# A fused conditional residual kernel: a new order of the work on all five engines

## What is computed

```
x = x + (softmax(mask(tanh(x W1 + b1) v)) x) / count        # attention pooling, A = 128
x = x + layernorm(x + relu(x w1[lang] + b1) w2[lang] + b2[lang]) * gamma[lang] + beta[lang]
x = x + zX * lap_columns(x) + zY * lap_rows(x) + zR * x * (1 - x)
x = x + x W[cat] + b[cat]                                   # W[cat]: 512 x 512, 1 MB
```

## Time and profile before

| what | value |
|---|---|
| median of 3 runs | 1118.82 us (1113.79 to 1120.64) |
| the profiled execution | 1114.18 us, span 1112.4 us |
| PE busy | 1051.4 us, 95% |
| DVE busy | 961.6 us, 86% |
| POOL busy | 710.2 us, 64% |
| ACT busy | 495.7 us, 45% |

### The profile page before, as it was taken

The page is one execution under the profiler, slowest core; times in us unless marked ns, Lnnn a source line. Parts: engine busy times, 40 slices in busy tenths (PEclk is TensorE's granted clock), DMA queues, the critical chain, the costliest instruction groups (busy, mean ns, idle before and its releaser), DMA issues.

```text
span 1112.4 us, 23554 instructions
## 1 busy us (share of the span) xinstructions
PE 1051.4 (95%) x4892; PEld 658.1 (59%) x4892; DVE 961.6 (86%) x1965; ACT 495.7 (45%) x1410; POOL 710.2 (64%) x652
## 2 busy tenths in 40 slices
PE   2489999999999999999999999999999999999996
PEld 1356665665666556666666656665666565565652
DVE  3288998998899889999899999988998898998984
ACT  0244444444444444444454444444444444444441
POOL 0066667657667676667667666666766766766765
PEclk9999999999999999999999999999999999999999
DMA  9478888788888988877787778898888788888873
GB/s 382 179 219 260 272 244 257 235 235 236 281 247 237 308 257 265 233 212 228 237 249 223 224 233 266 254 276 242 253 246 259 234 264 249 273 267 219 251 232 113
DMA packets 136182, 273.95 MB, mean 246 GB/s; under 512 B 29288, under 2 KB 29296, under 8 KB 128496
## 3 DMA queue, kind: packets, MB, share of 16 engines
q1 hardware_dynamic: 97600, 202.45, 60.2%
q10 hardware_dynamic: 38448, 70.01, 20.8%
HBM read 248.26 MB, written 33.55 MB: 253 GB/s over the span
## 4 chain that ended last, share of the span: by engine, by line
issue 32%; POOL 31%; PE 24%; DVE 9%; DMA 2%; DVEq 1%; POOLq 0%; ACT 0%; ACTq 0%; SPq 0%
POOL b_wide L817 12%; PE ps_out L390 10%; POOL neighbours L798 7%; POOL react L804 6%; POOL rstd L790 4%; DVE x L709 4%; PE bank_hidden L344 3%; PE ps_attn L322 3%; PE ps_adapt L372 3%; PE ps_pool L363 2%; DVE res L684 2%; DMA xts<-in_xT 2%; POOL above L810 2%; PE ps_x3T L380 1%; PE bank_scores L333 1%
## 5 line engine op out<-in xcount | busy, mean ns | idle before, releaser
L390 PE MATMUL ps_out<-w3s,x3T 128*128 x1024 | 489.5, 601 | 2.3 <-ACT x3T L441 2.3
L810 POOL TENSOR_TENSOR above<-above,below 128x512 f32<-128x512 f32 x128 | 164.6, 1286 | 255.8 <-DMA above<-x 255.3
L390 PEld LDWEIGHTS ps_out<-w3s,x3T 128*128 128x128 f32 x1024 | 185.2, 191 | 189.7 <-issue 188.1
L709 DVE SCALAR_TENSOR_TENSOR x<-above,zy_t,react 128x512 f32<-128x512 f32 x128 | 209.4, 1636 | 10.5 <-POOL above L810 8.9
L804 POOL TENSOR_TENSOR react<-react,x 128x512 f32<-128x512 f32 x128 | 179.8, 1405 | 2.1 <-ACT react L484 2.1
L817 POOL TENSOR_TENSOR b_wide<-b_wide,x 128x512 f32<-128x512 f32 x128 | 178.0, 1391 | 1.8 <-DMA b_wide<-in_b 1.8
L344 PE MATMUL bank_hidden<-w_all,xts 128*128 x1024 | 137.7, 278 | 23.6 <-DMA xts<-in_xT 23.6
L344 PEld LDWEIGHTS bank_hidden<-w_all,xts 128*128 128x128 f32 x1024 | 125.1, 193 | 54.1 <-issue 52.4
L790 POOL TENSOR_TENSOR rstd<-var_eps,minus_half 128x1 f32<-128x1 f32 x128 | 69.9, 546 | 133.1 <-DVE var_eps L676 133.1
L462 ACT ACTIVATE square_junk<-ps_adapt,neg_mean 128x512 f32<-128x512 f32 x128 | 88.0, 688 | 133.7 <-DVE neg_mean L639 133.7
L372 PE MATMUL ps_adapt<-w_all,hid 128*128 x256 | 133.6, 604 | 12.5 <-DVE x L691 12.1
(11 more groups left out here) (97 smaller groups left out, 1252.1 us busy)
## 6 DMA issues: line engine op xcount, KB each, us to landing
w3s<-in_w SPq DMA_DIRECT2D x128, 1024.0 KB
xts<-in_xT ACTq DMA_DIRECT2D x128, 256.0 KB, 4.9
xs<-in_x ACTq DMA_DIRECT2D x128, 256.0 KB, 5.4
b_wide<-in_b SPq DMA_DIRECT2D x128, 256.0 KB, 4.7
out_x<-res SPq DMA_DIRECT2D x128, 256.0 KB, 3.3
below<-x SPq DMA_DIRECT2D x128, 252.0 KB
above<-x SPq DMA_DIRECT2D x128, 252.0 KB
below<-x SPq DMA_DIRECT2D x256, 2.0 KB
```

What stands on the lines that cost most here:

```text
L390: mm = pe.matmul(ps_out[j.ring(2)][:, :], x3T[:, j.ring(2), k * P:(k + 1) * P], w3s[:, bass.ds(wslot * (K * D) + k * D, D)], start=(k == 0 ...
L709: nc.vector.scalar_tensor_tensor(x3[:, q, :], above[:, q, :], zy_t[:, bass.ds(i.n, 1)], react[:, q, :], ALU.mult, ALU.add).then_inc(x3_rea ...
L810: nc.gpsimd.tensor_tensor(above[:, q, :], above[:, q, :], below[:, q, :], ALU.add).then_inc(rows_ready, 1)
```

## The change

Nothing is added to or taken from the work of the engines; what changes is the order in `slot` on all five, and with it how many slots lie between a step and its use. On PE attn_project(s) comes first and takes over the wait for the transposed item, the category product is split into steps 0 and 1 at the end of one slot and steps 2 and 3 early in the next, mix_transpose is one slot later than its scores, and adapter_up stands after pool and the x3 transposes. adapter_project now waits for the relu of the item just before, and adapter_hidden for its own item's xw. On ACT load_xT(s) is the first step of slot s instead of a step of slot s-1. On DVE normalize stays last, with add_rows right before it, add_columns comes early and one item later, add_beta late, result one item later. On POOL the slot begins with inverse_std. On SP the shifts come first, then the b3 load of the item before, the store one item later, and the category load last.

```diff
@@ -269,16 +269,18 @@
 
             def slot(s):
                 if s.inside(B):
+                    shift_rows(s)
+                if (s - 1).inside(B):
+                    cat_m1, = load_params(sp, CAT, 1, s - 1)
+                    load_b3(s - 1, cat_m1)
+                if (s - 3).inside(B):
+                    item_m3, = load_params(sp, ITEM, 1, s - 3)
+                    store(s - 3, item_m3)
+                if s.inside(B):
                     cat, fresh, wslot = load_params(sp, CAT, 3, s)
-                    shift_rows(s)
                     load_w3(s, cat, fresh, wslot)
-                if (s - 2).inside(B):
-                    item_m2, = load_params(sp, ITEM, 1, s - 2)
-                    store(s - 2, item_m2)
-                if s.inside(B):
-                    load_b3(s, cat)
-
-            run_slots(slot, 0, B + 1)
+
+            run_slots(slot, 0, B + 2)
             for r in range(2):
                 sp.wait_ge(res_out[r], 16 * (B // 2))
                 sp.wait_ge(w3_in[r], 16 * (B // 2))
@@ -314,6 +316,7 @@
 
             def attn_project(a):
                 r = a.ring(2)
+                pe.wait_ge(xT_in[r], a.dma())
                 if a.is_first:
                     pe.wait_ge(w1a_in, 16)
                 if a.is_at_least(1):
@@ -335,11 +338,10 @@
                           ).then_inc(scores_mm, 1)
 
             def adapter_project(s, lang):
-                pe.wait_ge(xT_in[s.ring(2)], s.dma())
                 if s.is_first:
                     pe.wait_ge(w1_in, 16)
-                if s.is_at_least(2):
-                    pe.wait_ge(relu_ready, s.upto(2))
+                if s.is_at_least(1):
+                    pe.wait_ge(relu_ready, s.upto(1))
                 for k in range(K):
                     mm = pe.matmul(ps_xw, xts[:, s.ring(2), k, :], w1_all[:, bass.ds(lang * (K * A) + k * A, A)],
                                    start=(k == 0), stop=(k == K - 1))
@@ -350,8 +352,7 @@
                 pe.transpose(ps_mixT, mix[:, c.ring(2), :], ident[:, :]).then_inc(mixT_mm, 1)
 
             def adapter_hidden(f):
-                if (f + 1).inside(B):
-                    pe.wait_ge(xw_ready, (f + 1).upto())
+                pe.wait_ge(xw_ready, f.upto())
                 pe.wait_ge(mixT_ready, f.upto())
                 pe.matmul(ps_hid, xw[:, f.ring(2), :], mixT[:, f.ring(2), :], start=True, stop=True
                           ).then_inc(hid_mm, 1)
@@ -393,36 +394,35 @@
                     mm.then_inc(out_mm, 1)
 
             def slot(s):
-                h, j = s - 1, s - 4
-                if h.inside(B):
-                    pool(h)
-                if s.inside(B):
-                    kind, = load_params(pe, KIND, 1, s)
+                h, i, j = s - 1, s - 4, s - 5
+                if s.inside(B):
+                    attn_project(s)
+                if h.inside(B):
+                    mix_transpose(h)
                 if j.inside(B):
                     wslot, = load_params(pe, WSLOT, 1, j)
-                if h.inside(B):
+                    category(j, wslot, range(2, K))
+                if s.inside(B):
+                    kind, = load_params(pe, KIND, 1, s)
+                if h.inside(B):
+                    adapter_hidden(h)
+                if s.inside(B):
+                    attn_scores(s, kind)
+                if h.inside(B):
+                    pool(h)
                     lang_m1, = load_params(pe, LANG, 1, h)
-                if s.inside(B):
-                    attn_scores(s, kind)
-                if j.inside(B):
-                    category(j, wslot, range(0, 1))
+                if i.inside(B):
+                    x3_transpose(i)
                 if h.inside(B):
                     adapter_up(h, lang_m1)
-                if j.inside(B):
-                    category(j, wslot, range(1, K))
-                if (s + 1).inside(B):
-                    lang_p1, = load_params(pe, LANG, 1, s + 1)
-                if s.inside(B):
-                    mix_transpose(s)
-                if (s + 1).inside(B):
-                    adapter_project(s + 1, lang_p1)
-                    attn_project(s + 1)
-                if (s - 3).inside(B):
-                    x3_transpose(s - 3)
-                if s.inside(B):
-                    adapter_hidden(s)
-
-            run_slots(slot, -1, B + 3)
+                if s.inside(B):
+                    lang, = load_params(pe, LANG, 1, s)
+                    adapter_project(s, lang)
+                if i.inside(B):
+                    wslot_next, = load_params(pe, WSLOT, 1, i)
+                    category(i, wslot_next, range(0, 2))
+
+            run_slots(slot, 0, B + 4)
 
 
         @block.scalar
@@ -517,32 +517,31 @@
                 act.dma_start(xs[:, r], x[bass.ds(item, 1)].rearrange("o s d -> s (o d)")).then_inc(x_in[r], 16)
 
             def slot(s):
+                if s.inside(B):
+                    item, = load_params(act, ITEM, 1, s)
+                    load_xT(s, item)
+                if (s - 2).inside(B):
+                    lang_m2, = load_params(act, LANG, 1, s - 2)
+                    relu(s - 2, lang_m2)
                 if (s - 1).inside(B):
                     exponentials(s - 1)
+                if (s - 5).inside(B):
+                    move_x3T(s - 5)
+                if s.inside(B):
+                    load_x(s, item)
                 if (s - 3).inside(B):
                     reaction(s - 3)
-                if (s + 1).inside(B):
-                    item_p1, = load_params(act, ITEM, 1, s + 1)
-                    load_xT(s + 1, item_p1)
+                if (s - 2).inside(B):
+                    variance(s - 2)
                 if (s - 3).inside(B):
                     column_ends(s - 3)
-                if s.inside(B):
-                    item, = load_params(act, ITEM, 1, s)
-                    load_x(s, item)
-                if (s - 2).inside(B):
-                    variance(s - 2)
                 if (s - 1).inside(B):
+                    move_xw(s - 1)
                     move_mixT(s - 1)
                 if s.inside(B):
-                    move_xw(s)
                     attn_tanh(s)
-                if (s - 4).inside(B):
-                    move_x3T(s - 4)
-                if (s - 1).inside(B):
-                    lang_m1, = load_params(act, LANG, 1, s - 1)
-                    relu(s - 1, lang_m1)
-
-            run_slots(slot, -1, B + 3)
+
+            run_slots(slot, 0, B + 4)
 
 
         @block.vector
@@ -730,30 +729,30 @@
                     row_max(s)
                 if h.inside(B):
                     add_b2(h, lang)
+                if (s - 3).inside(B):
+                    add_columns(s - 3)
+                if s.inside(B):
+                    denominator(s)
+                if h.inside(B):
+                    add_adapted(h)
+                if s.inside(B):
+                    row_scale(s)
+                if h.inside(B):
+                    mean(h)
+                if s.inside(B):
+                    mix_rows(s)
+                if (s - 5).inside(B):
+                    result(s - 5)
+                if h.inside(B):
                     add_beta(h, lang)
-                if s.inside(B):
-                    denominator(s)
-                if h.inside(B):
-                    add_adapted(h)
-                if s.inside(B):
-                    row_scale(s)
-                if h.inside(B):
-                    mean(h)
-                if s.inside(B):
-                    mix_rows(s)
+                    add_epsilon(h)
+                    center(h, lang)
                 if (s - 3).inside(B):
                     add_rows(s - 3)
-                if (s - 4).inside(B):
-                    result(s - 4)
-                if h.inside(B):
-                    add_epsilon(h)
-                    center(h, lang)
-                if (s - 2).inside(B):
-                    add_columns(s - 2)
                 if h.inside(B):
                     normalize(h)
 
-            run_slots(slot, 0, B + 3)
+            run_slots(slot, 0, B + 4)
 
 
         @block.gpsimd
@@ -818,18 +817,17 @@
                                         ).then_inc(x3_b3_ready, 1)
 
             def slot(s):
+                if s.inside(B):
+                    inverse_std(s)
+                    sum_columns(s)
                 if (s - 2).inside(B):
-                    sum_rows(s - 2)
+                    add_b3(s - 2)
                 if (s - 1).inside(B):
-                    sum_columns(s - 1)
-                if (s - 3).inside(B):
-                    add_b3(s - 3)
-                if (s - 1).inside(B):
-                    react_times_x2(s - 1)
-                if s.inside(B):
-                    inverse_std(s)
-
-            run_slots(slot, 0, B + 2)
+                    sum_rows(s - 1)
+                if s.inside(B):
+                    react_times_x2(s)
+
+            run_slots(slot, 0, B + 1)
 
 
```

(18 more changed lines are left out.)

4 lines of the change are left out of this document (2 added, 2 removed).

## The result

The changed kernel takes 1196.93 us in the median of 4 runs (1190.72 to 1204.69), the one before 1119.59 beside it: 1.07 times as long, with a 95% interval of 1.0648 to 1.0751. The forecast was 1100, with a range up to 1122.

What follows compares the result with a forecast made beforehand. TensorE was taken as the bound, 8.04 us a slot, losing 19.9 us to DVE's order. 1114.2 - 25.7 = 1088.5; + 3.5 (xT) + 5.5 (b3, lock) = 1097.5, plus about half of 4.6: 1100 us, range 1088 to 1122.

Steps and rivals of the forecast that it cites:

- the frame of the change part by part: New slot timed from attn_project's start on PE; SP and PE load one index more, PE's floor stays 8.04 us.
- The b3 chain: SP's late b3 load delays POOL's add_b3; free in most slots, at its edge behind a new category.
- rival 3: b3 chain costs 0.4 us in each of 55 slots: 1114, or 1105 to 1110; 0.23 shared by three rivals.
- the lock: DVE and POOL instructions exclude each other: add_rows gains 1.0 us, add_columns and mix lose up to 1.0 each.
- The walk: Step-by-step timing of the new slots; over four slots 8.95, 7.6, 7.2 and 7.6 us, mean 7.8.
- The 19.9 us: TensorE's loss over 122 loop slots, read from adapter_up's wait for DVE's normalize; the change was to remove it.
- The floor: Sum of TensorE's work in one slot, 8.04 us, every piece kept by the change.
- The sum without losses: 1114.2 less 25.7 us for loop, head and tail: 1088.5, before the xT, b3 and lock costs.
- The room of adapter_up: On PE, normalize ends 1.7 us before adapter_up needs it, now about 0.5; its wait under 4 us in all.
- The xT load: load_xT issued later, landing free up to 6.2 us before attn_project on PE stops; 3.5 us taken.
- rival 1: xT becomes the bound: slot 8.45 us at a typical landing of 6.6, about 1138 us; chance 0.11.
- rival 2: DVE becomes the bound, two locks in every slot, 8.24 us: about 1113; 0.23 shared by three rivals.

Runs made afterwards that it cites:

- e9: Changed kernel with two whole copies for the six shifts and b3 loaded for the first two items only: 1090.85 us, ratio 0.9755.
- e5: Changed kernel with one parameter load per slot on SP instead of three: 1130.68 us, ratio 1.0137.
- e12: Changed kernel with one parameter load per slot on SP, three b3 buffers and load_b3 ahead of the shifts: 1097.26 us, ratio 0.9786.
- e4: Kernel before with two whole copies of 128 rows for the six shifts: 1100.86 us, ratio 0.9842.
- e14: Kernel before with two whole copies for the six shifts and b3 loaded for the first two items only: 1097.71 us, ratio 0.9808.
- e6: Kernel before with one parameter load per slot on SP instead of two: 1107.64 us, ratio 0.9931.
- e10: Kernel before with one parameter load per slot and four shifts (127 rows and one edge row each way) instead of six: 3289.86 us, ratio 2.9438.
- e7: Kernel before with one parameter load per slot on SP and the four one-row shifts issued by ACT: 1154.79 us, ratio 1.0388.

## Why the prediction was wrong

**The step that failed** is in the frame of the change part by part: "SP and PE load one index more per slot, in their sequencers", at a price of nothing. For PE that holds: with its extra load it reaches 8.04 a slot in e9, with nothing lost. SP does nothing but load and issue, and there the load counts in full; the statement ahead of the prediction that nothing is added to the work of the engines leaves it out too (384 parameter loads on SP for 256). SP's slot was never summed: 606.76 to 614.44 is 7.68, and the mean without waits 8.06, with two loads in it that no row of the forecast showed. With the third it is 8.57, and 122 x (8.57 - 8.04) = 65 us; 54 to 66 by the runs. What was taken was the issue time of the six shifts, as a delay of b3 inside a slot, not as a share of a stream that repeats.

The Trainium skill (DMA: Bandwidth & Descriptors, "Latency and other measured facts") gives `tensor_load` a floor of some 600 ns. On SP the median here is 716, which bears the size out, but the least is 266, under that floor, and there the measurement decides. As an estimate from the page's figure, the third load would have made SP's 8.06 into 8.7.

**The b3 chain** (rival 3) was seen with its right mechanism and undersized. It was put at 5.5 us with the lock, 22 at most. In e5, where SP has time, the loop loses 35.8, and the third buffer takes 30.7 of them away (e12). The walk had SP stand in load_w3's wait, start the shifts at 3.8 and issue b3 8.6 to 9.2 us into a slot. In the slot after the one above, attn_project starts at 658.52 by PE's timeline, x2 ends at 3.6 instead of 2.6, the shifts start at 5.2 (663.69), and b3, of 669.19, is at 10.7. SP is hardly ever in load_w3's wait (3.2 us in the whole loop): it comes to the shifts late from its own stream, the last parameter load of 1.28 in front. Landings were within (4.1 in the median; 7.97 in the stall above, issued at 580.86), but they came on top of an issue that was already late.

**The 19.9 us** were read as the cost of DVE's order, with adapter_up's wait as the proof. e4 and e14 refute that: with the old order and two copies for the shifts, 12 and 15.5 of them are gone, and that wait falls from 12.1 to 1.7 and 1.4. DVE's x2 was late since the shifts were late, two steps back: POOL's 255.3 us of waits for them fall to 24.0 and 4.1. The wait named the last link, not the first. SP's length alone explains only a part (4.9 in e6, where the six issues between x2 and the last shifted row stay). What the new order adds where SP and b3 are out of the way is small: e9 stands 6.9 us below e14, with intervals that just part; the four waits for the mix at the head (7.6 us in e14) are gone, as forecast.

**What was right.** The floor: 8.04 a slot, reached in e9. The sum without losses, 1088.5, stands against 1093.32 in e9's profiled execution: loop and tail come out as summed, and the 4.8 between are the head, where item 5's mix transpose is at 80.24 and not at 75.4, hardly sooner than before. The room of adapter_up: 0.8 us of waits in e12, forecast under 4. The xT load: PE waits 6.5 us for it in the loop, 3.5 were taken. In e5 it is PE's largest wait in the loop (9.6 us), but in e9 and e12 nothing is left of it there, so rival 1 falls. DVE's busy time of 901, under 962 and far from rival 2's 1010, with add_rows at its least of 0.74 in most items of e12. attn_project(1) at 42.13 against 42.2. Half right: item 5's mix transpose at 78.17 against 75.4, half the gain. Not as said: add_columns stays at 0.744 in the median, where 1.2 was expected, since POOL often stands idle beside it, waiting for b3; in e12 it is 0.946. And the forecast's own sign of being wrong, a usual slot above 8.15, came: 8.30. The tail took 35.3 us from the last mix transpose to the end, 31.3 were forecast: it is 30.6 in e12, so b3 and SP are late there too, though no run takes the tail apart.

**The miss in one line:** of the 98.8 us between the sum of 1097.5 and the profiled execution's 1196.3, 92 lie in the loop (a loss of 100.2, where 9.0 were allowed less 0.9 for the last item), 3 at the head, 4 at the tail.

## What to carry to other kernels

Sum the stream of every engine against the slot, and of the engine that only issues above all: its DMA issues (0.35 to 0.9 us each), its register loads and its arithmetic stand in no line of busy times. An engine at 8.06 us a slot beside a TensorE of 8.04, with few waits, is a second bound, and the first thing that a change of order must not lengthen. When a transfer is asked for at the end of a long stream and waits for its buffer, a third buffer and an earlier place can be worth more than a finer order of the engines that compute: here 33 us (e5 to e12) against 7 (e14 to e9).

## What the runs showed of the hardware that was not expected

- Rows decide the price of a shift out of proportion: the old order with the single load takes 1107.64 us with 126 rows (e6) and 3289.86 with 127 (e10), and rows come up to 21.9 us late. The price doesn't show at the issue of the first 127 rows (0.74 us) but at the two issues behind it (7.82 and 11.91), the latter of one row. The Trainium skill (DMA: Bandwidth & Descriptors, "Why a DMA increments its semaphore by 16 and not by 1") says that a transfer is spread over the largest number of engines up to 16 that divides its rows, which makes 14 of 126 and 1 of 127. The trace fits that (the same bytes at 83 GB/s over the span of e10, 246 before), though it doesn't show the engines one by one.
- A parameter load on SP costs 0.27 to 1.4 us for one to three numbers in the changed kernel, on PE and ACT mostly 0.3 (0.308 and 0.283 in the median). One load of four has a median of 1.07 us in e6 and 1.11 in e5, and still SP's stream is 0.6 us shorter than with two separate ones (e6 against the kernel before) and 0.95 shorter than with three (e5 against the changed kernel).
- A one-column POOL instruction can double: rstd takes 0.547 us before and 0.995 in the median after, where it meets add_rows on DVE, as here:

```profile
659.83 1.07 DVE L708 SCALAR_TENSOR_TENSOR x<-above,zy_t,react 128x512 f32<-128x512 f32 x1
```

```profile
660.32 0.99 POOL L789 TENSOR_TENSOR rstd<-var_eps,minus_half 128x1 f32<-128x1 f32 x1
```

It starts 0.58 before add_rows ends and lasts 0.44 longer than alone, and normalize stands behind it (54.4 us of waits for rstd). The forecast let the lock stretch only DVE's side. In e12, where x2 and b3 are in time, rstd is back at 0.547.
- An instruction of ACT doesn't start while an issue ahead of it is under way: two one-row transfers of 2 KB keep `column_ends` back for 1.10 us and take 1.16, more than a 512-column activation (0.80). An instruction that has already started runs on beside the issue: the `reaction` that starts at 604.80 in e7 lasts 0.80, and load_xT's issue begins at 605.05.
